# A transformer block with a final norm on one core: order of the transfers and of the reciprocal steps on SyncE

## The reference

```python
x = x + a_alpha * attention(ada_rmsnorm(x, t, gamma, beta), W_q, W_k, W_v, W_o)      # 16 heads of 16
x = x + f_alpha * swiglu(ada_rmsnorm(x, t, gamma2, beta2), gate_w, hidden_w, out_w, out_b)   # 1024 hidden
out = (x - mean) * rsqrt(var + 1e-5) * weight + bias
out = (out + tanh(t @ lin_w.T + lin_b)) * weight + bias
```

## Time and profile before

| what | value |
|---|---|
| time of 3 runs, us | median 783.85, 781.42 to 784.1 |
| the profiled execution: time, span, us | 783.73, 781.9 |
| mean granted clock of TensorE | 0.976 of full speed |
| PE busy, us, share of the span | 720.6, 92% |
| DVE busy | 536.7, 69% |
| ACT busy | 470.4, 60% |
| POOL busy | 390.7, 50% |

### The profile page before, as it was taken

How to read it: one execution, slowest core, us unless ns; L and a number is a source line. 1 busy time by engine, 2 the same in 40 slices (tenths; PEclk the granted TensorE clock), 3 DMA queues, 4 the chain that set the end, 5 groups by cost and what they waited for, 6 DMA issues and landing times.

```text
span 781.9 us, 17472 instructions
## 1 busy us (share of the span) xinstructions
PE 720.6 (92%) x6646; PEld 489.4 (63%) x6646; DVE 536.7 (69%) x795; ACT 470.4 (60%) x858; POOL 390.7 (50%) x491
## 2 busy tenths in 40 slices
PE   3778687899999999999999999999999999999995
PEld 3423243456776667775676667776677667678895
DVE  3477666668677676777667776768667776436765
ACT  3337666678566756677566756667666665753431
POOL 3325323354248553665448553766447453872433
PEclk9769989999999999999999999999999999999998
DMA  7854655446442544445442544445443540242110
GB/s 193 267 193 149 194 187 185 171 124 210 132 155 69 207 146 138 149 137 181 134 164 76 194 156 138 135 137 157 140 154 104 166 144 15 58 115 64 48 50 28
DMA packets 63500, 108.74 MB, mean 139 GB/s; under 512 B 10193, under 2 KB 17801, under 8 KB 63417
## 3 DMA queue, kind: packets, MB, share of 16 engines
q1 hardware_dynamic: 62744, 106.91, 43.3%
q10 hardware_dynamic: 544, 0.52, 0.2%
q0 software_dynamic: 128, 0.20, 0.1%
HBM read 59.60 MB, written 39.09 MB: 126 GB/s over the span
## 4 chain that ended last, share of the span: by engine, by line
PE 71%; DVE 10%; DMA 7%; issue 6%; ACT 4%; SPq 2%; POOL 1%; POOLq 0%; DVEq 0%; ACTq 0%
PE ps_x L1304 16%; PE ps_j L1194 11%; PE ps_o L1277 11%; PE ps_j L1317 9%; PE ps_s L1264 9%; PE ps_m L1249 6%; DVE mx L1016 4%; ACT prob L823 2%; DMA out_scratch<-o_raw 2%; PE ps_o L1317 2%; DMA qs<-m_hl 2%; DVE fx L982 2%; DVE gate_t L1056 1%; PE ps_m L1304 1%; PE ps_s L1304 1%
## 5 line engine op out<-in xcount | busy, mean ns | idle before, releaser
L1016 DVE TENSOR_REDUCE mx<-ps_m 128x2 f32<-128x1024 f32 x222 | 271.7, 1224 | 128.7 <-PE ps_m L1249 128.3
L823 ACT ACTIVATE prob<-ps_s 128x1024 f32<-128x1024 f32 x256 | 261.9, 1023 | 83.2 <-PE ps_s L1264 82.6
L1264 PE MATMUL ps_s<-qs,ks 64*128 64x512 f32 x512 | 120.6, 467 | 22.1 <-ACT prob L823 14.0
L1277 PE MATMUL ps_o<-prob,v 128*32 128x512 f32 x1024 | 138.4, 613 | 0.2 <-ACT o_raw L831 0.2
L1264 PEld LDWEIGHTS ps_s<-qs,ks 64*128 64x128 f32 x512 | 48.7, 186 | 141.1 <-issue 75.5
L1249 PE MATMUL ps_m<-ks,qs 64*128 64x512 f32 x444 | 94.2, 420 | 9.5 <-DVE mx L1016 5.5
L1304 PE MATMUL ps_x<-n,gh_hi 64*128 64x256 f32 x872 | 97.8, 284 | 1.7 <-DVE act_y L1063 1.6
L546 POOL TENSOR_TENSOR a_lo<-act_y,a_hi 128x256 fp32r<-128x256 f32 x100 | 73.4, 734 | 46.4 <-ACT a_hi L854 46.2
L1304 PE MATMUL ps_x<-n_x,gh_hi 64*128 64x256 f32 x872 | 94.4, 276 | 0.0
L571 POOL TENSOR_TENSOR xr<-xr,sc 128x512 f32<-128x512 f32 x41 | 53.1, 1296 | 64.6 <-DVE sc L1028 40.5
L1304 PEld LDWEIGHTS ps_x<-n,gh_hi 64*128 64x128 f32 x872 | 74.3, 184 | 13.7 <-DVE act_y L1063 10.2
(11 more groups left out here) (178 smaller groups left out, 1439.1 us busy)
## 6 DMA issues: line engine op xcount, KB each, us to landing
qs<-stack_scratch SPq DMA_DIRECT2D x32, 512.0 KB, 4.2
ks<-stack_scratch SPq DMA_DIRECT2D x32, 512.0 KB, 6.0
stack_scratch<-qk_hi SPq DMA_DIRECT2D x56, 256.0 KB, 3.3
out_scratch<-o_raw SPq DMA_DIRECT2D x32, 256.0 KB, 3.3
n_x<-n SPq DMA_DIRECT2D x32, 256.0 KB, 3.7
stack_scratch<-qk_lo SPq DMA_DIRECT2D x28, 256.0 KB, 3.6
xa<-in_x SPq DMA_DIRECT2D x8, 512.0 KB, 5.5
on_lo<-out_scratch SPq DMA_DIRECT2D x16, 256.0 KB
```

The source lines that it names most:

```text
L823: act.activation(prob[:, n % 2, 2 * h:2 * h + 2, :], ps_s[:], ACT.Exp, scale=SCALE).then_inc(p_r, 1)
L1016: dve.tensor_reduce(mx[:, group % 2, :, h, qt], max_pair(mp)[:], AX.X, ALU.max).then_inc(mx_red, 1)
L1264: mm = pe.matmul(ps_s[:, s, :], ks[r:r + 64, g, j, kb * P:(kb + 1) * P], qs[r:r + 64, g, j, :], start=True, stop=True)
L1277: mm = pe.matmul(ps_o[32 * i:32 * i + 32, :], v[:, g, kb, i, :], prob[:, n % 2, i, :], start=(kb == 0), stop=(kb == TT - 1), skip_group_ch ...
```

## The change

On SyncE, `max_rows` is put first in its unit. `o_read` moves from u1 to u2 and from u9 to u10, to stand behind `max_rows`. `store`, `load_tab_b` and `swap_halves` of u2, and `swap_halves` of u10, keep their unit, and now stand behind both. `rec_write` and `rec_read` move from u3 to u4 and from u11 to u12, behind the transfers of `stack_write`. On DVE the first `o_recip` moves from u2 to u3 (the one at u11 stays). On POOL and ACT `o_norm`, `o_low` and `o_high` move by one unit. The steps of the last sequence that fall behind unit 128 keep their places. No operation is added or removed.

```diff
@@ SyncE
-                if at(1, -1):
+                if at(2, 0):
+                    max_rows(b, 1)
+                if at(2, -1):
                     o_read(b - 1, 1)
                 if at(2, -3):
                     store(b - 3, 1)
                 if at(2, -2):
                     load_tab_b(b - 2)
                 if job_at(n - 1) and job_at(n - 1)[:2] == ("FT", 1):
                     swap_halves(job_at(n - 1)[2], 1)
-                if at(2, 0):
-                    max_rows(b, 1)
-                if at(3, -1):
+                if at(3, -1) and n > NU:
                     rec_write(b - 1, 1)
                     rec_read(b - 1, 1)
+                if at(3, -1):
                     load_xr(b - 1, 1)
                 if at(3, 1):
                     stack_write(b + 1, 0)
+                if at(4, -1) and n < NU:
+                    rec_write(b - 1, 1)
+                    rec_read(b - 1, 1)
...
-                if at(9, 0):
+                if at(10, 0):
+                    max_rows(b, 3)
+                if at(10, 0):
                     o_read(b, 0)
                 if at(10, -1):
                     swap_halves(b - 1, 0)
-                if at(10, 0):
-                    max_rows(b, 3)
-                if at(11, 0):
+                if at(11, 1):
+                    stack_write(b + 1, 2)
+                if at(12, 0):
                     rec_write(b, 0)
                     rec_read(b, 0)
-                if at(11, 1):
-                    stack_write(b + 1, 2)
@@ GpSimd
-                if at(4, -1):
+                if at(4 if n > NU else 5, -1):
                     o_norm(b - 1, 1)
-                if at(13, 0):
+                if at(14, 0):
                     o_norm(b, 0)
-                if at(5, -1):
+                if at(5 if n > NU else 6, -1):
                     o_low(b - 1, 1)
-                if at(14, 0):
+                if at(15, 0):
                     o_low(b, 0)
@@ VectorE
-                if at(2, -1):
+                if at(2 if n > NU else 3, -1):
                     o_recip(b - 1, 1)
```

More of the change, by code:

```diff
@@ L435, in unit @@
                     stack_write(b + 1, 1)
+                if at(6, 0):
+                    max_rows(b, 2)
                 if at(7, 1):
                     stack_read(b + 1, 0)
-                if at(6, 0):
-                    max_rows(b, 2)
                 if at(8, 1):
```

## The result

The changed kernel takes 840.38 us (median of 4 runs, 838.62 to 843.67), the one before 783.98 us (4 runs, 781.42 to 786.54). The ratio is 1.0733 with a 95% interval of 1.0703 to 1.0763. The direction is the one forecast; the size is not: 840.4 us stands outside the range of 783 to 812.

A forecast was written before the change was run, and what follows sets the result against it. TensorE was taken to bound the kernel, busy 16.00 of 16 us in the dense middle. The sum was 783.7 - 7.6 (gain) + 14.4 (u4 stalls) + 7.3 (u12 stalls) = 797.8 us, range 783 to 812.

The forecast's parts named there:

- The gain: Start of the kernel: earlier max rows save 3.1 us at 96 us, 1.9 at 130 us and 2.6 of lower clock, 7.6 us.
- The reciprocal steps at no price: Reciprocals, writes, reads, norms and casts run one unit later on DVE, SyncE, POOL and ACT; cost taken as nothing.
- The moment of issue of the swap: On SyncE in block 3, the swap's second half is issued at 291.08 us at u2, 334.15 us at u10.
- The landing: Swap's second half, issue to TensorE's load: 5.2 us at u2, 4.2 at u10; stalls of 2.4 and 0.5 us in block 3.
- the 21.7: Forecast TensorE stalls for late swaps, in us: 14.4 at u4 of six blocks plus 7.3 at u12.
- the crowded case: Block 7's swap behind `on_lo`, `out_y`, `tab_b`: landing 4.9 us, 5.2 to the load; all swaps crowded gives 804.8 us.
- The quiet case: Swap at 730.1 us on an idle queue: landing 3.6 us, 3.9 to the load; all swaps quiet gives 787.9 us.
- C: Rival: the stalls bring TensorE's lower clock; if eight did, 819 us; chance 0.10.
- A: Rival: the swaps land in time and only the gain is left, 776.1 us; chance 0.14.
- B: Rival: TensorE makes up half of the 21.7 us of stalls, 787.0 us; chance 0.14.
- The promised rows: Profile signs: 11 to 13 `n_x` waits, 17 to 28 us, longest 2 to 3.5; `m_hl` wait about 3.1 us.

## Why the prediction was right and wrong

**The gain.** Forecast 7.6 us, measured 8.6 us where the dense middle begins, and 10.2 us where nothing takes it back (the kernel with the swap in front, 774.08 us, against 784.27 for the one before in its comparison). The max rows at u10 of block 0 leave SyncE 1.9 us earlier, at 89.33 us, and the clock behind them is at full speed. Right, a little small: before, TensorE ran at half speed for 3.4 us once more, from 143 us, with no wait over 1 us in the 12 us ahead of it, and the units from 142.94 to 148.40 us took 1.2 us longer than they do now. The forecast did not see that stretch. It is the moved reads that bring the gain: with only the reads moved, 2.1 us of the wait for the max rows are left, while neither the swap's move alone nor the reciprocals' alone changes the 8.1 us by more than 0.2 us.

**The reciprocal steps at no price.** Right: no new wait of ACT for `d_c` (one of 2.8 us, 3.0 before), TensorE's waits have no row for it, and the run with them alone is at 1.0007. POOL waits 94.1 us in 9 times for `d_c` where it waited 91.4 in 16, and neither ACT nor TensorE waits longer for what POOL makes of it.

**The moment of issue of the swap.** Right: forecast 291.08 us with the unit u2 starting where it did; measured from the start of the unit it is 10.7 us against 10.8, and at u10 9.7 us against 9.9.

**The landing: the step that failed.** The working said "I take 5.2" for u2 and "4.2 to the load" for u10. The second transfer lands after 6.5 us at u2, and TensorE's load starts right behind it; at u10 it is 5.9 us. Those are 1.3 and 1.7 us more. The waits follow: at u4 2.88 to 4.49 us, 3.7 in the mean, for the 2.4 forecast; at u12 of blocks 2 to 6 1.90 to 2.16 us, 2.0 in the mean, for 0.5; in blocks 1 and 7 3.64 and 4.56 us for 2.3 and 2.5. The sum of 22.0 + 18.4 = 40.4 us replaces the 21.7. The row of 4.9 us was read as the crowded case, but there the read of `on_lo` stood 2.4 us ahead of the first half of the swap, at the new place 1.7 us at u2 and 0.7 us at u10. At u10 I let the crowd go, since `out_y` and `tab_b` were absent; the two runs on what stands ahead show that `on_lo` by itself adds 2.1 us there, and that the other two add nothing behind it. The quiet case was well sized, 3.7 to 4.1 us, but by luck: the 3.6 us of the earlier trace rows is the median of the pair (3.3 and 3.9 us), so the second transfer alone took 3.9 us, and the load came 0.04 us behind its landing and not 0.3. Likewise the second transfer of the earlier trace rows was issued at 634.5 us, and the crowded case was 4.9 us to the load, not 5.2; read rightly, it would have been 0.3 us further off.

**The clock: priced as a rival.** C had a chance of 0.10 and counted eight stalls. The reason against it was the wait of 2.34 us at 130 us with full clock behind it. The forecast itself put the clock behind the stalls at nothing. In the dense middle, waits of 1.90 us and up were followed by the lower level 12 times in 13. One case in a sparse stretch was no evidence for the dense one; at the same place, in the run with the reciprocal steps alone, a wait of 3.22 us was followed by it. The run with repeated passes shows at least 18.2 us of it. C's own number was 819 us; with 40.4 us of waits and some 23 us of clock it comes to 783.7 - 7.6 + 40.4 + 23 = 839.5 us. The forecast would have needed both corrections: the landing alone gives 783.7 - 7.6 + 40.4 = 816.5 us.

**A and B.** A is excluded by the 13 waits, and with it the time of 777.1 us by the fixed part of a transfer in the Trainium skill's page DMA: Bandwidth & Descriptors (section Anatomy of one DMA): no swap here landed in 2.0 us, the quickest transfer of one took 3.0. That page's figure is for transfers that GpSimd issues; SyncE issues these. B failed: no stretch behind a wait is shorter than before, and at most the 27.3 - 22.9 = 4.4 us by which the lower clock cost less than its upper bound can have been made up.

**The promised rows.** 13 waits, as said; 40.4 us in total, not 17 to 28; the longest 4.6, not 3.5 at most. `n_x` is issued 3.5 us after `m_hl`. The max rows' wait fell to 2.2 us, where about 3.1 was said. The window from 96 us is at 1.00.

Still open: why the read of `on_lo` holds up the transfers behind it by more than its bytes, and what beyond the length of a wait decides whether the lower clock follows. In the run with `on_lo` behind the swap, waits of 1.72, 2.38 and 3.21 us were followed by it, those of 1.05 to 1.14 and one of 1.89 us were not; in the run with one swap late, one of 2.62 us was not.

## What to carry to other kernels

On an engine that issues all transfers in order, give the first place in a unit to what the bound engine reads soonest, and count for each transfer behind it three things: the wait that is now ahead of it, the issue time of every transfer passed, and the landing behind a large DRAM read, which here took 5.8 to 7.0 us where it took 3.7 to 4.1 with the reads behind. When a change puts waits like these, of 1.9 to 4.6 us, into a stretch where TensorE is always busy, price the lower clock behind each one as part of the forecast, not as a rival: here it added 23 us to 40. And when an edit made of several moves loses, try the moves apart; here one place that costs 66 us covered moves that together win 10.

## What was not expected of the hardware

- The landing of the swap depended on what stood ahead of it in the same queue and not on the same reads behind it. At u10 of block 3 it took 3.7 us with two reads issued within 2 us behind it, 5.9 us with the same reads ahead, and 3.8 us with only the 16 KB one ahead.
- Waits of 1.90 to 4.56 us in a busy stretch were followed by 3.4 or 6.8 us at 1.2 GHz in 12 of 13 cases, and the stretch behind such a wait was 1.1 to 3.1 us longer than before. Useless matmuls during the wait made the kernel 18.2 us faster.
